# FFN weights decoded in the first token tile of the FFN stage instead of in the state-space loop

## The reference

```python
x = L0_attn_u                                            # (4, 1024, 512)
x = x + layernorm(mamba(layernorm(x), W_in, conv_w, conv_b, W_out, A_log, D_param, dt_bias))
x = x + layernorm(ffn(layernorm(x), lut, gate_idx, up_idx, down_idx))

def ffn(x, lut, gate_idx, up_idx, down_idx):
    gate = x @ lut[gate_idx].T        # gate_idx, up_idx: (1376, 512) codes 0..15
    up   = x @ lut[up_idx].T
    return (silu(gate) * up) @ lut[down_idx].T           # down_idx: (512, 1376)
```

## Time and profile before

| | |
|---|---|
| median of 3 runs | 1589.3 us (1588.49 to 1592.45) |
| the profiled execution, span | 1590.2 us |
| stage 1, from the start to the barrier | about 873 us |
| stage 2 | about 717 us |
| PE busy over the span | 1431.8 us (90%) |
| DVE busy | 1034.1 us (65%) |
| ACT busy | 592.3 us (37%) |
| POOL busy | 541.7 us (34%) |
| DMA | 65.22 MB, mean 41 GB/s |

### The profile page before, as it was taken

The page is one execution under the profiler, slowest core; times in us unless marked ns, Lnnn a source line. Parts: engine busy times, 40 slices in busy tenths (PEclk is TensorE's granted clock), DMA queues, the critical chain, the costliest instruction groups (busy, mean ns, idle before and its releaser), DMA issues. The chain is left out here.

```text
span 1590.2 us, 23447 instructions
## 1 busy us (share of the span) xinstructions
PE 1431.8 (90%) x7392; PEld 707.9 (45%) x7392; DVE 1034.1 (65%) x2288; ACT 592.3 (37%) x1046; POOL 541.7 (34%) x653
## 2 busy tenths in 40 slices
PE   3798897898979988899886999999999999999998
PEld 1354443443535434445443444444444444444443
DVE  6799797897886978969885535435363545445333
ACT  4365554654645546555453221203020221213020
POOL 1275655556465555665754001010101001010101
PEclk9899998998999999989998999999999999999999
DMA  5011122022121221112201101010100101010000
GB/s 168 1 49 49 49 62 64 15 72 59 38 63 36 62 62 49 59 39 62 62 22 59 53 9 46 1 55 1 54 1 21 34 7 47 1 53 1 27 1 27
DMA packets 37454, 65.22 MB, mean 41 GB/s; under 512 B 5056, under 2 KB 15296, under 8 KB 37312
## 3 DMA queue, kind: packets, MB, share of 16 engines
q1 hardware_dynamic: 35424, 63.47, 12.7%
q10 hardware_dynamic: 1888, 0.03, 0.1%
HBM read 46.71 MB, written 16.78 MB: 40 GB/s over the span
## 5 line engine op out<-in xcount | busy, mean ns | idle before, releaser
L1386 ACT ACTIVATE gtanh<-bank,c_gate_half 128x512 f32<-128x512 f32 (+1 forms) x88 | 60.4, 687 | 537.0 <-PE bank L1421 537.0
L1421 PE MATMUL bank<-xt,ffn_hi 128*128 128x512 f16 (+1 forms) x704 | 213.8, 386 | 13.4 <-DVEq L82 6.7
L991 DVE TENSOR_SCALAR mask<-codes_h 128x416 f16<-128x416 f16 x640 | 215.5, 368 | 1.9
L1421 PE MATMUL bank<-xt_odd,ffn_hi 128*128 128x512 f16 (+1 forms) x704 | 209.4, 379 | 0.0
L1359 POOL TENSOR_TENSOR drstd<-dvar,neg_half 128x1 f32<-128x1 f32 x32 | 17.4, 545 | 481.1 <-DVE dvar L1518 481.1
L828 PE MATMUL bank<-mask,diag 128*128 128x416 f16 x640 | 133.2, 353 | 46.8 <-DVE mask L991 46.6
L1493 DVE SCALAR_TENSOR_TENSOR gsilu<-gtanh,bank 128x512 f32<-128x512 f32 (+1 forms) x88 | 60.5, 687 | 137.6 <-ACT gtanh L1386 137.4
L1421 PE MATMUL bank<-xt,ffn_lo 128*128 128x512 f16 (+1 forms) x352 | 135.7, 385 | 0.0
L1445 PE MATMUL bank<-ffn_hi,h_hi 128*128 128x512 f16 (+1 forms) x352 | 133.5, 379 | 0.0
L1421 PE MATMUL bank<-xt_odd,ffn_lo 128*128 128x512 f16 (+1 forms) x352 | 133.4, 379 | 0.0
L1445 PE MATMUL bank<-ffn_hi,h_lo 128*128 128x512 f16 (+1 forms) x352 | 133.3, 379 | 0.0
(11 more groups left out here) (184 smaller groups left out, 2768.3 us busy)
## 6 DMA issues: line engine op xcount, KB each, us to landing
codes_sb<-codes SPq DMA_DIRECT2D x80, 208.0 KB, 3.5
ut<-u SPq DMA_DIRECT2D x8, 1024.0 KB, 5.7
ures<-u SPq DMA_DIRECT2D x32, 256.0 KB, 2.7
x_scratch<-x SPq DMA_DIRECT2D x32, 256.0 KB, 2.0
xf<-x_scratch SPq DMA_DIRECT2D x8, 1024.0 KB, 5.9
out<-res SPq DMA_DIRECT2D x32, 256.0 KB, 2.0
ffn_hi<-w_in_t SPq DMA_DIRECT2D x4, 580.0 KB, 10.3
ffn_hi<-w_out_t SPq DMA_DIRECT2D x1, 1024.0 KB, 14.5
```

What stands on the lines that cost most here:

```text
L991: ins = nc.vector.tensor_scalar(mask[:, n, q, :], codes_h[:, n, :], float(2 * q), None, ALU.is_equal)
L1386: gtanh_ready.inc(nc.scalar.activation(gtanh[0:w, m % 2, :], banks[2 + m % 2][0:w, :], ACT.Tanh, scale=c_gate_half[0:w, :]))
L1421: last = nc.tensor.matmul(bank, wt[:, c0:c0 + w], xts[i][:, half, k, :], start=(k == 0 and n == 0), stop=(k == KC - 1 and n == 2))
```

## The change

- Stage 1 no longer decodes: no loads of codes except for the first two units, no casts on POOL, no masks, no decode matmuls, no copies into the FFN weights. `outputs` and `time_steps` keep their steps, with nothing between them. The shared banks serve 14 uses a tile instead of 24.
- The table of diagonals is made by DVE at the end of stage 1 instead of in its prologue. With it comes `pair_code`, a column of 8 values per partition (2q, and 2q + 1 in the lower 64 partitions). A mask now compares with that column, a per-partition scalar read from memory, and the codes need no lowering.
- There are 33 units of 512 columns instead of 40 of 416: for each block m of INTER its gate columns, its up columns and its down rows (the last gate and up unit have 384 columns). Units 0 and 1 are loaded in stage 1's prologue and cast at its end.
- In stage 2 the first token tile decodes. Before block 0 PE decodes units 0 to 2, and ahead of each block m it decodes units 3m+3 to 3m+5, those of the next block. The masks are put into DVE's queue and the casts and the copies out into ACT's. The first two tiles are written out ahead of the loop, which now runs twice.
- A gate or up unit is loaded by four DMAs (rows of 512 bytes), a down unit by two. The decode uses banks 6 and 7.
- The tile `gsilu` is gone; its product is written over `gtanh`.

```diff
-UNIT = 416
-TILE_UNITS = 5
+UNIT = D
+UNITS = [(kind, m) for m in range(MB) for kind in (GATE, UP, DOWN)]
...
+        def codes_to_half(eng, u):
+            w = unit_width(u)
+            eng.wait_ge(s_codes[u % 2], codes_landed(u))
+            nc.scalar.activation(codes_h[:, u % 2, :, 0:w], codes_sb[:, u % 2, :, 0:w], ACT.Copy).then_inc(s_half, 1)
...
                 def tiles(eng, body):
-                with eng.Fori(0, TILES // 2 - 1) as pair:
+                for i in range(2):
+                    body(i, i, 0, True)
+                with eng.Fori(1, TILES // 2 - 1) as pair:
...
                 @block.sync
+                    for u in range(2, len(UNITS)):
+                        sp.wait_ge(s_half, u - 1)
+                        load_codes(sp, u)
...
                 @block.scalar
+                    def to_half(u):
+                        if u < len(UNITS):
+                            act.wait_ge(s_masks, GROUPS * (u - 1))
+                            codes_to_half(act, u)
+                    def evacuate(u):
+                        for n in range(2):
+                            act.wait_ge(s_decoded, 2 * u + n + 1)
+                            for w, lo in ((ffn_hi, 0), (ffn_lo, NST)):
...
+                                ins = nc.scalar.activation(decoded_rows(w, u, n), src, ACT.Copy)
+                            ins.then_inc(s_weights, 1)
...
+                        if first:
+                            to_half(2)
+                            for u in range(3):
+                                evacuate(u)
+                                to_half(u + 3)
                         for m in range(MB):
+                            if first:
+                                for u in range(3 * m + 3, min(3 * m + 6, len(UNITS))):
+                                    evacuate(u)
+                                    if u < 3 * m + 5:
+                                        to_half(u + 3)
...                         # gate's tanh of block m, high part of block m - 1
+                            if first:
+                                to_half(3 * m + 8)
...
                 @block.tensor
+                    def decode(u):
+                        for n in range(2):
+                            if u >= 1:
+                                pe.wait_ge(s_weights, 2 * (u - 1) + n + 1)
+                            for q in range(PAIRS):
+                                if q % GROUP == 0:
+                                    pe.wait_ge(s_masks, GROUPS * u + 2 * n + q // GROUP + 1)
+                                last = nc.tensor.matmul(banks[6 + n][:, 0:width], ...)
...
                         for m in range(MB):
+                            if first:
+                                for u in range(3 * m + 3, min(3 * m + 6, len(UNITS))):
+                                    decode(u)
+                                pe.wait_ge(s_weights, 2 * (3 * m + 2))
...
                 @block.vector
+                    def masks(u):
+                        dve.wait_ge(s_half, u + 1)
+                        for n in range(2):
+                            for q in range(PAIRS):
+                                if u >= 1 and q == 0:
+                                    dve.wait_ge(s_masks_used, 2 * (u - 1) + n + 1)
+                                elif u >= 1 and q == GROUP:
+                                    dve.wait_ge(s_decoded, 2 * (u - 1) + n + 1)
+                                ins = nc.vector.tensor_scalar(mask[:, n, q, 0:width], codes_h[:, u % 2, n, 0:width],
+                                                              pair_code[:, q:q + 1], None, ALU.is_equal)
...
+                        if first:
+                            for u in range(6):
+                                masks(u)
                         for m in range(MB):
+                            if first and 3 * m + 6 < len(UNITS):
+                                masks(3 * m + 6)
...                         # the two products and the low part; next_stats or next_split
+                            if first:
+                                for u in range(3 * m + 7, min(3 * m + 9, len(UNITS))):
+                                    masks(u)
```

More of the change, by code:

```diff
@@ L765, in _ @@
                     iterations(act, body)
+                    for u in range(2):
+                        codes_to_half(act, u)
                 @block.tensor
                 def _(pe):
-                    masks_used.start(pe)
                     def take(n):
@@ L818, in project_z @@
                             for w, n in ((win_hi, 0), (win_lo, 0), (win_hi, 1))]))
-                    def decode(t, k, more):
-                        for n in range(2):
-                            b = bank_of(f"D{k}" + "'" * n, more)[:, 0:UNIT]
-                            take(use(t, f"D{k}" + "'" * n, more))
-                            for q in range(PAIRS):
-                                if q % GROUP == 0:
-                                    pe.wait_ge(masks_ready.sem, masks_ready.now(
-                                        t, k * GROUPS + n * (GROUPS // 2) + q // GROUP + 1))
-                                last = nc.tensor.matmul(b, diag[:, q].rearrange("p n m -> p (n m)"), mask[:, n, q, :],
-                                                        start=(q == 0), stop=(q == PAIRS - 1))
-                                if q == GROUP - 1:
-                                    masks_used.inc(last)
-                            filled.inc(last)
                     def prepare(t, half, c):
@@ L926, in body @@
                         segment_sums(t, 2)
-                        decode(t, 1, more)
                         input_transpose(t, 2, more)
@@ L940, in body @@
                         transpose_y(t, 2)
-                        decode(t, 2, more)
                         if more:
@@ L1125, in outputs @@
                             ysplit[:, 1, :], y[:], yq[:], ysplit[:, 0, :], ALU.mult, ALU.subtract))
-                        if unit is not None:
-                            masks(row, half, unit, more, first=YSTEPS + 1)
                     def out_stats(t, c):
@@ L1142, in body @@
                         decayed(t, 0)
-                        masks(row, half, 0)
-                        outputs(t, half, row, 0)
+                        outputs(t, half, 0)
                         ln_split(i, 0)
@@ L1148, in body @@
                         decayed(t, 1)
-                        outputs(t, half, row, 1, 1, more)
+                        outputs(t, half, 1)
                         ln_split(i, 2)
@@ L1154, in body @@
                         decayed(t, 2)
-                        outputs(t, half, row, 2, 2, more)
+                        outputs(t, half, 2)
                         if more:
@@ L1168, in body @@
                             conv_silu(i, p, 2)
-                        outputs(t, half, row, 3, 3, more)
+                        outputs(t, half, 3)
                         if more:
@@ L1174, in body @@
                             conv(i, 3)
-                            time_steps(i, p, lambda j: one_mask(row, half, 4, j))
-                            masks(row, half, 4, first=15)
-                        else:
-                            masks(row, half, 4, more)
+                            time_steps(i, p)
                         out_stats(t, 3)
@@ L1235, in _ @@
                     step(nc.vector.tensor_scalar(c_down[:], c_down[:], expo[:, 2:3], None, ALU.mult))
+                    low_half(3)
+                    for f in range(FB):
+                        if f >= 1:
+                            conv_silu(0, 0, f - 1)
+                        conv(0, f)
+                        if f == 1:
+                            time_steps(0, 0)
+                    conv_silu(0, 0, FB - 1)
+                    ln_stats(1)
+                    iterations(dve, body)
                     step(nc.vector.tensor_scalar(lut_s[:], lut_sb[:], wscale[:, 2:3], None, ALU.mult))
```

186 lines of the change are left out of this document (78 added, 108 removed).

## The result

The changed kernel takes **1645.2 us** (median of 4 runs, 1643.1 to 1647.3) against 1589.2 for the kernel before (4 runs): ratio 1.0351, 95% interval 1.0337 to 1.0366. I had forecast 1606 and a range that ended at 1636. The direction is right and the size is wrong: 56 us slower instead of 17.

The account below looks back on a forecast made before the run. PE bounds stage 2; in stage 1 neither PE nor DVE is full and they pass work round a ring. 1590.2 - 123.4 + 143.5 - 3.3 = 1607.0 us span, median 1606, range 1568 to 1636.

Parts of the forecast that it names:

- Sum: 15.2 us a tile: Stage 1, first seven tiles: saving from removing DVE's masks and lowerings, 12.1 + 2.1 + 5.2 - 4.2 us a tile.
- The term of 5.2 us: Stage 1: hidden masks are held up while POOL works; 0.11 us of that saved for each, 5.2 us a tile.
- Last tile, 14.5: Last tile of stage 1: loses the same masks but has no conv to wait for, 14.5 us less.
- Prologue, 2.5: Stage 1's prologue: the diagonals' 4.2 us leave it, counted as 2.5 us less.
- The first FFN tile, +143.5: Stage 2, first tile, which now decodes: 232.4 us against 88.9, 143.5 us more.
- the 3 us for the low clock: First FFN tile: two losses to a low granted clock on PE, from gaps of 1 to 2.4 us, make 3 us.
- Rival 2: First FFN tile: masks cost 0.215 us or less, PE bounds blocks at 15.6, start 28.5; total 1592 us; chance 0.13.
- Rival 3: First FFN tile: scalar from memory takes masks out of fast mode, 0.45 us each; total 1683 us; chance 0.05.
- Rival 4: First FFN tile: loads don't keep up, start and blocks lengthen by 15 us; total 1622 us; chance 0.10.
- One back edge fewer, 3.3: FFN tiles behind the first: the loop has one back edge fewer, 3.3 us less.
- Rival 1: Stage 1 gives up nearly all of PE's share, 20.5 us a tile; total 1566 us; chance 0.22.
- The 4.2: Stage 1: unit 0's masks lie partly in a wait that remains, so 4.2 us a tile of them save nothing.

Follow-up runs that it names:

- e3: Kernel before without DVE's 80 masks and 5 lowerings a tile; PE's decode, ACT's copies and POOL's casts stay: 1482.2 us.
- e4: Kernel before without PE's decode and ACT's copies out; DVE's masks, lowerings and POOL's casts stay: 1618.2 us.
- e8: Changed kernel plus 8 useless matmuls of 416 columns at each of five places a stage-1 tile where the decode had been: 1622.5 us.
- e7: Changed kernel with its masks compared with a constant in the instruction instead of a scalar read from a tile: 1635.1 us.
- e11: Kernel before, loop over the FFN tiles as it was, plus 8 matmuls of 128 columns in the prologue: 1579.3 us.

## Why the prediction was wrong

**"Sum: 15.2 us a tile" is the step that failed.** 9.75 came. It failed twice.

First, **PE's share was put at nothing, and it is negative.** The sum was made of DVE's work alone, and its bounds (12.1 to 22.5) allowed only a gain from the decode's matmuls. I counted lost low clock in stage 2, 3 us, and in stage 1 not at all, although shows 0.95 for a tile in the middle and 0.89 for the last, which has the least for PE to do. The square of e3 and e4 prices the removal at 2.8 to 3.6 us a tile the wrong way, and e8 gives 3.0 back by putting useless matmuls in the gaps. That is 2.8 of the 5.45 us, by e3 against the changed kernel.

Second, **the held-up masks were worth less than counted.** e3, which keeps PE's decode and its clock, saves 12.55 us a tile by DVE's share alone; my sum for the same work was 15.2. The term of 5.2 us (0.11 for each of 47 hidden masks) stands against the low end, "the hold-ups by POOL fall on other DVE work instead", and by the rows half of it went that way. DVE's groups over five tiles of e3 (busy, mean ns), against the kernel before:

```profile
L1076 DVE TENSOR_TENSOR decay<-decay,gsb 128x1024 f32<-128x1024 f32 x20 | 30.4, 1518 | 16.7 <-ACT decay L648 16.6
L1009 DVE TENSOR_TENSOR xsplit<-ut,xsplit 128x512 f16<-128x512 f32 x20 | 23.2, 1199 | 0.9
L1109 DVE TENSOR_TENSOR y<-y,xd 128x512 f32<-128x512 f32 x20 | 18.3, 916 | 0.7
L1111 DVE TENSOR_TENSOR y<-y,zs 128x512 f32<-128x512 f32 x20 | 16.1, 803 | 0.7
```

```profile
L1079 DVE TENSOR_TENSOR decay<-decay,gsb 128x1024 f32<-128x1024 f32 x20 | 25.2, 1261 | 10.2 <-ACT decay L649 9.7
L1012 DVE TENSOR_TENSOR xsplit<-ut,xsplit 128x512 f16<-128x512 f32 x20 | 15.6, 822 | 0.4
L1112 DVE TENSOR_TENSOR y<-y,xd 128x512 f32<-128x512 f32 x20 | 13.7, 684 | 0.2
```

Four of each a tile: the decays 4 x 0.257, the splits of the input 4 x 0.377, y + xd 4 x 0.232 longer, y * zs 4 x 0.150 shorter (it was 953 ns): 2.9 us a tile of work that has become slower, where 2.65 are missing. My sign for this, a mean above 0.9 for y * zs in the changed kernel, failed (0.788), and the one for the last step of the split held (0.924): the hold-ups moved to other steps than I had named. A mean mixes two kinds. In e3, from 253 to 700 us, y + xd ran 5 times with POOL idle, each in 0.69 us, and 16 times beside work of POOL, 10 in 0.69 and 6 in 1.19 to 1.80. In the kernel before all 21 took 0.68 to 0.69. One of the long ones, with what POOL did:

```profile
352.81 1.76 DVE L1109 TENSOR_TENSOR y<-y,xd 128x512 f32<-128x512 f32 x1
...
352.76 1.27 POOL L452 TENSOR_TENSOR zs<-zs,ztanh 128x512 f32<-128x512 f32 x1
353.97 1.34 POOL L413 CAST codes_h<-codes_sb 128x832 f16<-128x832 int32 x1
```

The second half of the split of y (0.103 longer) and the last step of the conv (0.131) add 0.9, not all of it on the path. All of the steps named here read two tiles in SBUF. The Trainium skill, page "SBUF — State Buffer", section "Who interferes with whom", has it that a DVE instruction with two inputs in SBUF contends with GpSimd's reads; the rows fit, since steps with an input in PSUM stay at 0.68 to 0.69. Without POOL's casts, in the changed kernel, the decays (1382 ns), the splits (1018) and y + xd (854) are shorter than in e3. That these microseconds are the missing 2.65 is an account from rows; no run took POOL's work away with the rest unchanged.

**Last tile, 14.5.** 7.3 came. The clock in it was 0.82 in the changed kernel; before it was 0.89. That it is the same cause, with less work on PE to cover the waits, fits, but no run was read for it. **Prologue, 2.5:** 1.6.

**The first FFN tile, +143.5.** 143.9, and its mechanism holds. The chain of the changed kernel there:

```profile
798.03 9.44 DMA codes_sb<-codes
...
824.42 0.63 DVE mask L1458 x2
825.07 1.06 ACT codes_h L201
826.15 0.59 ACT ffn_hi L1321
826.75 0.60 ACT ffn_lo L1321
827.40 3.63 PE bank L1380 x16
831.02 5.18 PE bank L1411 x24
...
843.84 3.63 PE bank L1380 x16
847.46 5.20 PE bank L1411 x24
```

The decode of unit 5 ends 34.6 us behind the barrier (forecast 32.5), the first block takes 847.46 - 831.02 = 16.4 (16.0), the second 16.8 (16.5), one with a split 18.5 (18.2), with the statistics 19.7 (19.7). Start and nine blocks are 2.1 and 1.3 us over, and the 3 us for the low clock, of which 1.8 are seen in the start (8 decode matmuls take 3.61 us there, 16 later ones 3.63), make up for them: the half microsecond is in part luck. Mask to cast to the two copies to the third decode is the chain that I had named, and it is that of blocks 0 to 2 and 7. The masks' pace is 0.264 where I took 0.25 between 0.215 and 0.338; e7 puts the constant ones at 0.217. Rival 2's blocks would have been right with constants, its start 5 us too short (e7). Rival 3 needed 0.28 a mask and was only 0.016 away. Rival 4: behind the start no load is on the chain; in the start the codes landed at 807.47, 11.1 us behind the barrier (I had said 10).

**"One back edge fewer, 3.3."** 11.3 came. The price was taken from one gap of 3.44; the second gap of the kernel before (3.23) and the low clock behind either (32.94 us for the run of 144 matmuls that takes 31.08 at full clock, and 33.98 behind the second) weren't counted: 3.44 + 1.86 + 3.23 + 2.90 = 11.4. And the reason was wrong: e11 is without gaps with both back edges, so it doesn't take the peeling.

**Rival 1** wanted 84 us a tile or less. It took PE's waits and work to be on the path. e3, with all of PE's decode in place, is at 89.7, and e4 shows that PE's part alone gives nothing, so it was never near.

Why the range missed too: its low bound for stage 1 (95 us) lay 18 us above what came. No case had a removed matmul costing time. And the bound of 12.1 a tile isn't the sum without its 5.2, which is 12.1 + 2.1 - 4.2 = 10.0: with it the bound would have been 80 us, and the upper end of the range some 15 us above 1636. (The 4.2 itself is 490.86 - 487.11 = 3.75 by the rows that it names.)

## What to carry to other kernels

Before taking work off an engine whose clock depends on being busy, look at what fills its waits afterwards: if it was the removed work, the removal can cost time, and its bound must reach below zero. Where several engines pass the work round, price a removal engine by engine, by leaving out one engine's share at a time; and don't count on getting back the time for which an operation is held up by another engine by removing the operation: here, by the rows, other steps were held up in its place. The best kernels here are the one before with its first FFN tiles peeled or 8 small matmuls more in the prologue (1583.4 and 1582.7 us, 0.4% faster); none that decodes in the FFN stage came below 1622.

## What the runs showed of the hardware that I had not expected

- 40 matmuls a tile whose results nobody reads made the kernel 22.7 us faster (e8 1622.5 against 1645.2), the granted clock rising from 0.88 to 0.94. Twice as many gave 4.6 us in a single execution, hardly more than the scatter.
- Idle times of PE of 3.0 us in the midst of dense work were followed by the lower clock level, one of 1.3 us wasn't (rows of e8 above); four of 0.5 to 1.9 us close together were (kernel before, 566.6 to 574.0 us).
- The same 2913 matmuls of seven tiles were busy for 558 us at a clock of 0.88 and for 598 at 0.82.
- DVE's step y + xd took 0.69 us whenever POOL was idle, and up to 1.80 beside some of POOL's operations (e3).
- A compare of 512 float16 columns with a scalar from a tile takes 0.264 us, with a constant 0.217.
- The gaps of 3.44 and 3.23 us at back edges of the unchanged kernel were in no other kernel, among them one that differs by 8 matmuls in the prologue. Their cause stays open.
